# Eight of 39 expert tiles taken from a table of the first 11 sequences, in one program with grouped attention

## The reference

```python
h = hidden_states + attn_out
out = h + moe(rmsnorm(h, norm2_w), gate_w, w1, w3, w2)
# moe: logits = xt @ gate_w; topv, topi = top_k(logits, 2); probs = softmax(topv)
for e in range(E):
    h = jax.nn.silu(xt @ w1[e]) * (xt @ w3[e])
    out = out + w[:, e:e + 1] * (h @ w2[e])
```

## Time and profile before

| | |
|---|---|
| median of 3 runs | 1260.15 us (1258.65 to 1260.41) |
| the profiled execution | 1259.27 us |
| its span (first to last instruction) | 1257.2 us |
| busy share of the span, PE / DVE / POOL / ACT | 91% / 62% / 48% / 44% |
| mean clock granted to PE | 0.972 of full speed |
| start of step 16 of grouped attention on PE | 974.66 us |
| last matmul of grouped attention (`count`) | 1016.30 us |
| first matmul of the experts | 1025.64 us |
| last matmul of the experts | ends at 1247.5 us |

### The profile page before, as it was taken

One profiled execution on the slowest core, in us unless ns is written; L12 is line 12 of the kernel. 1 busy time (PEld: TensorE's weight loads), 2 busy tenths in 40 slices (PEclk: granted clock), 3 DMA queues, 4 the chain that ended last, 5 costly groups with the idle time before them and its releaser, 6 DMA issues. The chain is left out here.

```text
span 1257.2 us, 26135 instructions
## 1 busy us (share of the span) xinstructions
PE 1144.3 (91%) x8173; PEld 882.4 (70%) x8174; DVE 775.7 (62%) x1914; ACT 549.3 (44%) x1466; POOL 603.2 (48%) x752
## 2 busy tenths in 40 slices
PE   8998989969999799879999999999999849999996
PEld 5775556635555434358887888888888639999996
DVE  5555788868888589936667667767766432222221
ACT  3444766643333100036666666566666412222221
POOL 2003565536555467455566666656665312233233
PEclk9999999999999889979999999999999869999998
DMA  7000000008994040030000000000000038888884
GB/s 280 0 1 9 14 18 13 9 2 179 205 206 86 1 173 1 1 138 1 5 14 14 18 14 13 21 13 13 13 14 18 21 130 235 232 241 237 235 243 98
DMA packets 57268, 99.86 MB, mean 79 GB/s; under 512 B 5808, under 2 KB 44016, under 8 KB 56432
## 3 DMA queue, kind: packets, MB, share of 16 engines
q1 hardware_dynamic: 48048, 83.37, 23.6%
q0 software_dynamic: 7152, 9.34, 4.3%
q10 hardware_dynamic: 2000, 6.29, 1.3%
HBM read 87.53 MB, written 30.48 MB: 94 GB/s over the span
## 5 line engine op out<-in xcount | busy, mean ns | idle before, releaser
L1922 PEld LDWEIGHTS ga.pkq<-ga.xnT,g.early 128*128 128x128 f32 x1280 | 151.4, 193 | 9.6 <-issue 8.2
L1922 PE MATMUL ga.pkq<-ga.xnT,g.early 128*128 128x128 f32 x1280 | 156.8, 276 | 1.0 <-ACT ga.halves L1840 1.0
L1699 POOL TENSOR_TENSOR ga.halves<-ga.halves,g.ga_sinT 128x512 f32<-128x512 f32 x80 | 103.0, 1287 | 53.0 <-ACT ga.halves L1840 53.0
L1966 PE MATMUL ga.turn_out<-g.early,ga.aT 128*128 128x256 f32 x512 | 117.0, 382 | 0.5 <-ACT ga.aT L1862 0.5
L1847 ACT ACTIVATE ga.e<-ga.psc,ga.negmax 128x128 f32<-128x128 f32 x256 | 90.4, 365 | 48.7 <-DVE ga.negmax L1768 47.7
L1707 POOL TENSOR_TENSOR ga.kqT<-ga.by_cos,ga.halves 128x512 f32<-128x512 f32 x80 | 102.2, 1278 | 15.9 <-issue 15.9
L1966 PEld LDWEIGHTS ga.turn_out<-g.early,ga.aT 128*128 128x128 f32 x512 | 94.9, 190 | 12.3 <-ACT ga.aT L1862 0.7
L1755 DVE TENSOR_TENSOR ga.by_cos<-ga.pkq,g.ga_cosT 128x512 f32<-128x512 f32 x80 | 55.3, 691 | 74.3 <-PE ga.pkq L1922 43.3
L2081 DVE TENSOR_TENSOR ex.hT<-ex.silu,ex.p 128x512 f32<-128x512 f32 x39 | 26.8, 688 | 112.2 <-PE ex.p L2132 106.4
L2125 PEld LDWEIGHTS ex.p<-ex.xnT,ex.w 128*128 128x128 f32 x624 | 77.3, 195 | 5.5 <-issue 2.6
L2125 PE MATMUL ex.p<-ex.xnT,ex.w 128*128 128x128 f32 x624 | 77.8, 279 | 3.0 <-DMA ex.w<-in_mo_w 2.2
(11 more groups left out here) (289 smaller groups left out, 2586.7 us busy)
## 6 DMA issues: line engine op xcount, KB each, us to landing
ex.w<-in_mo_w SPq DMA_DIRECT2D x78, 512.0 KB, 4.5
mo_rows<-in_pad_rows SPq DMA_DIRECT2D x1, 18447.0 KB, 100.9
ex.row<-mo_rows SPq DMA_DIRECT2D x39, 129.0 KB, 3.3
g.late<-in_mo_w SPq DMA_DIRECT2D x1, 4096.0 KB, 12.3
g.ctxT<-in_ctxR SPq DMA_DIRECT2D x1, 2048.0 KB, 13.3
xa.ctxT<-in_ctxT SPq DMA_DIRECT2D x16, 128.0 KB, 2.5
g.spare<-cv_rows SPq DMA_DIRECT2D x1, 2048.0 KB, 8.2
g.early<-in_ga_wq ACTq DMA_DIRECT2D x1, 2048.0 KB, 7.9
```

What stands on the lines that cost most here:

```text
L1699: nc.gpsimd.tensor_tensor(by_sin[:, par, :].rearrange("p (h t) -> p h t", h=REP), halves[:, par, :].rearrange("p (h t) -> p h t", h=REP), ...
L1922: last = nc.tensor.matmul(pkq[:, par, j * P:(j + 1) * P], w[:, q, at * P:(at + 1) * P], xnT[:, s.par, q, :], start=(q == 0), stop=(q == C ...
L1966: last = nc.tensor.matmul(pout, aT[:, h // REP, (h % REP) * P:(h % REP + 1) * P], g.ga_wo[:, h, :], start=(h == 0), stop=(h == H - 1))
```

## The change

Both stages become one program, `grouped_attention_and_experts`; `experts` now only returns the parts of each engine's work, which the attention's step functions call. The expert stage's buffers move into the idle memory `g.spare`, and its four PSUM areas are those of the attention (`p1` and `p3` are the two halves of `pkq`, `turn` and `py` those of `psc`).

In step 14, just before the rank of sequence 11 (they are numbered from 0), `count_early` counts the first 11 sequences, and `early_ends` and `early_tables` on DVE make a table for eight tiles that are certainly full by then. `tables` later makes the table for the other 31. SP loads tiles 0 and 1 once the early table is there, 2 and 3 between the last stores of the residual sums, 4 to 7 after them, and only then waits for the late table. PE's steps 16, 17 and 18 call parts of tiles 0 to 2 in between (`between` and `meet`). On ACT and DVE the order of the last softmax groups in step 16 is changed too.

```diff
+
+    last = at + (count - lead - at) // 2 * 2
+    with eng.Fori(at // 2, last // 2) as k:
         emit(At(2 * k, 0, count))
         emit(At(2 * k, 1, count))
     for s in range(last, count + lag):
...
+EARLY, EARLY_B = 8, 11
+assert EARLY <= (2 * P * EARLY_B - E * (P - 1) + P - 1) // P
 ROW = D + 2
+EX_SIZE = 4 * C * F + 2 * F + 4 * D + 2 * ROW + F
 
...
-        sp.dma_start(g.acc[bass.ts(s.i, P), :], g.x[:, s.i, :]).then_inc(self.acc_stored, 16)
+        stored = self.acc_late if s.base is None and s.n >= B - 2 else self.acc_stored
+        sp.dma_start(g.acc[bass.ts(s.i, P), :], g.x[:, s.i, :]).then_inc(stored, 16)
 
...
 
-    def end_sends(self, pool):
+    def early_rows_sent(self, sp):
...
-            pool.wait_ge(self.sent[k], 16 * B)
+            sp.wait_ge(self.sent[k], 32 * ((EARLY_B + 1 - k) // 2))
+
+    def rows_sent(self, sp):
+        for k in range(2):
+            sp.wait_ge(self.sent[k], 16 * B)
...
+        nc = self.nc
         src, dst = tiles, self.ends
         for shift in (1, 2, 4):
             nc.vector.tensor_copy(dst[:, 0:shift], src[:, 0:shift])
             nc.vector.tensor_tensor(dst[:, shift:], src[:, shift:], src[:, 0:E - shift], ALU.add)
             dve.drain()
             src, dst = dst, (self.ends2 if dst is self.ends else self.ends)
-        nc.vector.tensor_tensor(past, spread(self.tile_no[:], 2, E), spread(src[:], 1, TILES), ALU.is_ge)
-        dve.drain()
...
+        dve.drain()
+        nc.vector.tensor_scalar(tiles[:], tiles[:], MAGIC, None, ALU.add)
+        dve.drain()
+        nc.vector.tensor_scalar(tiles[:], tiles[:], -MAGIC, None, ALU.add)
+        dve.drain()
+
+    def early_ends(self, dve):
+
+        dve.wait_ge(self.early_counted, 1)
+        self.rounded(dve, self.pearly, -63.5 / P)
+        self.ends_of(dve, self.tiles)
+
+    def early_tables(self, dve):
+
+        nc, g, n = self.nc, self.g, EARLY
+        tiles, ends, past, expert_f, start_f = self.tiles, self.ends, self.past[:, 0:EARLY, :], self.expert_f[:, 0:EARLY], self.start_f[:, 0:EARLY]
...
+        nc.vector.tensor_tensor(past, spread(self.tile_no[:, 0:n], 2, E), spread(ends[:], 1, n), ALU.is_ge)
+        nc.vector.tensor_tensor(self.used[:], tiles[:], ends[:], ALU.subtract)
+        dve.drain()
+        nc.vector.tensor_reduce(expert_f, past, AX.X, ALU.add)
+        nc.vector.tensor_scalar(self.used[:], self.used[:], float(n), 0.0, ALU.add, ALU.max)
...
+
+    def tables(self, dve):
+
...
+        nc, g, n = self.nc, self.g, TILES - EARLY
+        tiles, used, step, past = self.tiles, self.used, self.step, self.past[:, 0:TILES - EARLY, :]
+        expert_f, start_f = self.expert_f[:, 0:n], self.start_f[:, 0:n]
...
+        nc.vector.tensor_copy(g.tile_row[:, EARLY:], start_f)
+        nc.vector.tensor_copy(g.tile_expert[:, EARLY:], expert_f).then_inc(self.table, 1)
...
+    def count_early(self, pe):
+        pe.wait_ge(self.slot_ready, EARLY_B)
+        pe.wait_ge(self.chosen_ready, EARLY_B + 1)
+        self.nc.tensor.matmul(self.pearly, self.ones[:], self.earlier[:], start=True, stop=True).then_inc(self.early_counted, 1)
+
...
+            steps(sp, step, 0, 0, count=B - 4, first=2)
+            load = ex_load(sp)
+            router.early_rows_sent(sp)
+            sp.wait_ge(router.early_table, 1)
+            load(At(None, 0, TILES))
+            load(At(None, 1, TILES))
+            step(At(None, B - 4))
+            step(At(None, B - 3))
+            step(At(None, B - 2))
+            load(At(None, 2, TILES))
+            load(At(None, 3, TILES))
+            step(At(None, B - 1))
+            for t in range(4, EARLY):
+                load(At(None, t, TILES))
+            router.rows_sent(sp)
+            sp.wait_ge(router.table, 1)
+            steps_from(sp, load, EARLY, 0, 0, TILES)
+            sp.wait_ge(g.ex_added, 16 * TILES)
...
@@ -1719,6 +1805,8 @@
                     router.send(pool, d)
                 if a.on:
                     router.root(pool, a)
+                if s.base is None and s.n in (B + 1, B + 2):
+                    ex_step(At(None, s.n - B - 1, TILES))
...
             steps(pool, step, 2, 4)
-            router.end_sends(pool)
+            pool.wait_ge(router.acc_late, 32)
+            for k in range(2, 4):
+                ex_step(At(None, k, TILES))
+            steps_from(pool, ex_step, 4, 0, 1, TILES)
...
                 if c.on:
+                    if s.base is None and s.n == B + 2:
+                        scale_rows(At(None, 0, TILES))
+                        meta(At(None, 2, TILES))
                     router.choose(dve, c)
+                if s.base is None and s.n == B + 1:
+                    product(At(None, 0, TILES))
...
                 if c.on:
                     router.slots(dve, c)
+                if s.base is None and s.n == B - 2:
+                    router.early_ends(dve)
...
                 if b.on:
-                    normalise(b, 2)
-                    maxima(b, 3)
+                    if s.on:
+                        normalise(b, 2)
+                        maxima(b, 3)
+                    else:
+                        maxima(b, 3)
+                        normalise(b, 2)
                 if s.on:
...
+            silu, turned_rows = ex_scalar(act)
+
+            def ex_step(t):
+                n = t.back(-1)
+                if t.on:
+                    silu(t)
+                if n.on:
+                    turned_rows(n)
...
+                if s.base is None and s.n in (B, B + 2):
+                    turned_rows(At(None, s.n - B, TILES))
+                if s.base is None and s.n == B + 1:
+                    router.exp_margin(act, c)
+                    silu(At(None, 0, TILES))
+                if s.base is None and s.n in (B + 1, B + 2):
+                    silu(At(None, s.n - B, TILES))
...
+                    swap(s, 1)
+                elif b.on:
+                    copy_pT(b, 0)
+                    copy_aT(b, 0)
+                    copy_pT(b, 1)
+                    exps(b, 2)
+                    exps(b, 3)
+                if b.on:
                     copy_pT(b, 2)
                     copy_aT(b, 1)
+                if s.base is None and s.n == B:
+                    turned_rows(At(None, 1, TILES))
...
+            turned_rows(At(None, 3, TILES))
+            ex_step(At(None, 3, TILES))
+            steps_from(act, ex_step, 4, 1, 1, TILES)
...
+            def ex_step(t):
+                n, b = t.back(-1), t.back(1)
+                if t.on:
+                    first_product(t)
+                    second_product(t)
+                if n.on:
+                    turn_rows(n)
+                if b.on:
+                    last_product(b)
+
+            def turn_first():
+                pe.wait_ge(halves_ready, NB * B - 1)
+                turn_rows(slot(0), pkq[:, 0, :])
+
+            def first_of_first():
+                pe.wait_ge(halves_ready, NB * B)
+                first_product(slot(0))
+
+            def turn_second():
+                pe.wait_ge(e_ready, KV * B - 1)
+                turn_rows(slot(1))
+
+            def turn_second_and_product():
+                turn_second()
+                second_product(slot(0))
+
+            def second_slot():
+                first_product(slot(1))
+                second_product(slot(1))
+
+            def third_rows():
+                turn_rows(slot(2))
+                pe.wait_ge(e_ready, KV * B)
+                last_product(slot(0))
+
+            between = {B: (turn_first, first_of_first, turn_second_and_product),
+                       B + 1: (second_slot,),
+                       B + 2: (third_rows, lambda: first_product(slot(2)), lambda: second_product(slot(2)))}
+
             def step(s):
                 if s.base is None and s.n == 2:
                     pe.wait_ge(router.filled, 3)
                     pe.wait_ge(router.loaded, 16 * len(router.constants))
+                if s.base is None:
+                    s.others = list(between.get(s.n, ()))
                 a, b, c, n = s.back(2), s.back(1), s.back(3), s.back(-1)
                 if c.on:
+                    if s.base is None and s.n == B - 1:
+                        pe.wait_ge(router.early_table, 1)
                     router.turn_row(pe, c)
+                if s.base is None and s.n in (B, B + 2):
+                    s.meet()
...
                 if c.on:
+                    if s.base is None and s.n == B - 2:
+                        router.count_early(pe)
                     router.rank(pe, c)
+                if s.base is None and s.n > B:
+                    s.meet()
...
@@ -1984,6 +2191,8 @@
                         turn_probs(b, r)
                         if r < 2:
                             scores(b, r + 2)
+                        if r >= 1:
+                            s.meet()
```

367 lines of the change are left out of this document (200 added, 167 removed).

## The result

The changed kernel takes **1239.74 us** (median of 4 runs, 1238.27 to 1242.08), the kernel before, in the same comparison, 1260.01 (4 runs, 1258.65 to 1260.41): a ratio of 0.9843, 95% interval 0.9825 to 0.986, that is 20.3 us less. The prediction was 1235 (1229 to 1244), a gain of 24.5. The profiled execution of the changed kernel is the slowest of the four, 1242.08 with a span of 1240.2, so that the two spans differ by 17.0 us only.

What follows compares the result with a forecast made beforehand. PE was taken as the bound, with 31.4 us idle or slow before the steady tiles. 31.4 - 1.9 - 2.5 - 3.0 + 0.5 = 24.5 us off 1259.27 gives 1234.8, rounded to 1235, range 1229 to 1244.

Steps and rivals of the forecast that it cites:

- Idle and slow time from step 16 to tile 2: PE from step 16's start to tile 2's last product: 31.4 of 76.97 us idle or slow; 1.9 stays in step 16.
- what no row showed: Short waits on PE and time at 1.2 GHz that no row shows: 3.0 us taken, between 0 and 7.
- Rival 1: Steps 16 to 18 take tiles badly, PE stays at 1.2 GHz: about 12 us more stay, time 1247; chance 0.12.
- The early table: New DVE work of 3.85 us in step 14, delaying PE's step 15: cost 2.5 us, between 0 and 3.3.
- Late table, step 17, SP and POOL: Late table on DVE, step 17's row wait, loads and stores: cost 0, the table with about half a microsecond's margin.
- rival 2: The wait only moves: tile 8's rows come late, 12 us shown after tile 7, time about 1247; chance 0.03.
- Function tables on ACT: One table load of 1.28 us becomes three: 0 on the path, at most 1.3; by the skill 1.5 us worse.
- The adds: POOL's chain of adds starts earlier about as much as PE, and part of its backlog goes: gain 0.5 us.
- Rival 3: POOL's adds become the bound: at 6.86 us apart the time would be 1285, slower; chance 0.04.
- tile 2's last product ends near 1027: Sign of being right: on PE, tile 2's last product, at 1051.63 before, ends near 1027.
- PE's first row of step 15 waits 2 to 3 us: Sign of being right: PE's first row of step 15, sequence 12's, waits 2 to 3 us.
- no wait over 2 us: Sign of being right: no wait over 2 us on PE between 975 and tile 3.

Runs made afterwards that it cites:

- Experiment 7: Changed kernel with tiles 0 to 3 run behind step 18 on every engine, early table and SP's early loads kept; 1254.42 us.
- experiment 4: Changed kernel with `early_ends` moved directly ahead of `early_tables`, behind group 3's division in step 14; 1238.24 us.
- experiment 5: Changed kernel with one-operand instructions of the early table's first part turned into two-operand `tensor_tensor`; 1238.44 us.
- experiment 6: Changed kernel with each instruction of the early table's first part taking one operand from PSUM, five instructions more; 1239.60 us.
- experiment 2: Changed kernel with the early table's work moved to step 15's gap on DVE, the count's read staying in step 14; 1232.34 us, again 1230.97.
- the second profile: The changed kernel run again without alteration, beside other versions on one chip; 1237.86 us.
- Experiments 1: Changed kernel without computing the early table: DVE only waits for the count and writes a constant table in three short instructions; 1230.53 us.

## Why the prediction came out as it did

The range held the time, and the direction and the main mechanism were right. The gain was 20.3 instead of 24.5 us. By the terms of its sum:

- *Idle and slow time from step 16 to tile 2* (31.4, less 1.9 and 3.0 for what stays: 26.5). Measured 27.9. The waits that stay in step 16 are 0.26, 0.74 and 0.47, together 1.5 where 1.9 was taken; what no row showed came to 2.0 instead of 3.0, with the clock at 1.00 all through. Rival 1 is out. Experiment 7 shows that both halves were needed.
- *The early table* (2.5, between 0 and 3.3). Measured 7.3 and 8.5 in two profiles, outside both ends. **This is the step that failed.** Its price was taken from the slack at one place, DVE's row of sequence 12 against PE's turn of it, and the work was counted as 3.85 us. Three things were missing. First, `early_ends` stands ahead of group 2's maxima, behind which ACT's in-order queue holds its copy for group 1: a second chain, with a wait of its own (experiment 4 takes this wait away and leaves the other). Second, the work took 6.9 us, not 3.85: POOL's instructions hold up DVE's in SBUF (experiments 5 and 6; with POOL quiet, in experiment 2, it takes 4.1). The rows of 1.50 and 1.23 us stood among the quoted ones and were read as the cost of `rows`; in experiments 4 and 6, where POOL is quiet at that moment, the same lines take 0.61 and 0.17. Third, PE at half clock behind a wait, which the prediction charged to steps 16 to 18 and not to steps 14 and 15: 1.3 and 1.2 us in the two longest rows of the first profile; the second profile had full clock behind its second wait, so that part of this is luck. Experiments 1 and 2 show that the whole term belongs to this work in this place.
- *Late table, step 17, SP and POOL* (0). Right. DVE finishes the late table at 1041.0 and starts tile 4's product at 1041.14, and PE has no wait at tile 4, 5 or 8; rival 2 is out. It was close: that product ends at 1041.83, and PE's tile 5 needs its buffer at 1041.98, 0.15 us later where half a microsecond was reckoned.
- *Function tables on ACT* (0). Right: loads of 1.28 us each, no wait of PE behind them. The Trainium skill, "ScalarE: Activation LUTs", section "What ACT_TABLE_LOAD costs", counts about 2.66 us for a switch with its drain; no drain shows here, where the next activation starts within 0.02 us of two of the loads (the third is followed by a wait for DVE). By that figure the prediction reckoned an estimate of 1.5 us more. The three loads lay beside PE's work, and what they would cost on the path no run shows.
- *The adds* (0.5). Measured 0.1. Rival 3 is out: 5.42 us apart.

With 27.9, 0.1 and 7.3 to 8.5 the sum is 19.5 to 20.7 us, against 20.3 measured. That the range held the time is in part luck: the early table cost 4.8 to 6.0 us more than was taken, 1.4 us of it came back at the first term, and the rest used up room that was meant for tiles that fit badly into the last steps.

Of the signs named, "tile 2's last product ends near 1027" failed: it ended at 1034.67. "PE's first row of step 15 waits 2 to 3 us" came true (2.77), and no wait over 2 us followed after 975. The missing one was a wait at group 1's values in step 14.

## What to carry to other kernels

Before small work is put on an engine, list every chain that is queued behind that place, also on the engines that wait for it in order, and not just the one result that is named next. Look for a place where the engine idles and its partner is quiet: here one step later the same work left PE's time as in the kernel before (1.2 us above a kernel without the work), where it had cost 7 to 8 us. Rows eight times as long as their neighbours of the same size were here waiting for another engine, and their length was no price of the work.
